# Output projection of two convolution layers: one fp32 product, or three fp32r products of split operands

## The reference

```python
p = silu(x @ p_w.T + p_b); q = silu(x @ q_w.T + q_b); v = silu(x @ v_w.T + v_b)
a1 = rpe_mlp(pos, t1) * decay        # taps of a Toeplitz product along w, one set per channel
a2 = rpe_mlp(pos, t2) * decay        # the same along h
qv = q * v
out = p * (toeplitz_w(qv, a1) + toeplitz_h(qv, a2))
x = x + (out @ o_w.T + o_b)          # o_w: (192, 576); this product is what the change touches
```

## Time and profile before

| | us |
|---|---|
| median of the runs | 19111.07 |
| profiled execution | 19115.89 |
| its span | 19114.2 |
| PE busy | 14621.5 (76%) |
| DVE busy | 13659.7 (71%) |
| ACT busy | 9805.9 (51%) |
| POOL busy | 7607.1 (40%) |

### The profile page before, as it was taken

How to read it: one execution, slowest core, us unless ns; L and a number is a source line. 1 busy time by engine, 2 the same in 40 slices (tenths; PEclk the granted TensorE clock), 3 DMA queues, 4 the chain that set the end, 5 groups by cost and what they waited for, 6 DMA issues and landing times. The chain is left out here.

```text
span 19114.2 us, 278580 instructions
## 1 busy us (share of the span) xinstructions
PE 14621.5 (76%) x79256; PEld 8486.3 (44%) x79256; DVE 13659.7 (71%) x13058; ACT 9805.9 (51%) x14679; POOL 7607.1 (40%) x4057
## 2 busy tenths in 40 slices
PE   7899898989997677767676776677777667767789
PEld 5666666666665333333233333333333333333367
DVE  5666666666665788778688778688787688787732
ACT  4444444444443566565366556266665356665400
POOL 1000000000000477666366666177666366666500
PEclk9999999999998899999899999899999889999999
DMA  5222222222222000000100000100000100000011
GB/s 122 59 59 59 63 51 62 58 64 56 56 59 67 14 4 1 3 4 13 42 2 3 3 4 1 54 1 3 4 1 3 48 7 4 3 1 3 28 47 40
DMA packets 127667, 562.53 MB, mean 29 GB/s; under 512 B 20988, under 2 KB 81788, under 8 KB 105468
## 3 DMA queue, kind: packets, MB, share of 16 engines
q1 hardware_dynamic: 114780, 470.00, 10.0%
q0 software_dynamic: 12288, 86.71, 2.1%
HBM read 440.00 MB, written 126.27 MB: 30 GB/s over the span
## 5 line engine op out<-in xcount | busy, mean ns | idle before, releaser
L1156 POOL TENSOR_TENSOR L2.u<-L2.u 128x784 f32<-128x784 f32 x3072 | 5656.9, 1849 | 1821.7 <-PE L2.ps L1261 1233.6
L1261 PE MATMUL L2.ps<-L2.u,L2.ident 128*128 128x392 f32 x12288 | 4595.7, 499 | 129.4 <-DVE L2.y L1618 129.4
L1630 DVE TENSOR_TENSOR_SCAN L2.u<-L2.u,L2.state,L2.ps 128x784 f32<-128x784 f32 x2304 | 4163.1, 1834 | 175.5 <-ACT L2.ps L1413 146.9
L1419 ACT COPY L2.u<-L2.ps 128x784 f32<-128x784 f32 x3840 | 3102.9, 808 | 902.7 <-PE L2.ps L1230 895.9
L1230 PE MATMUL L2.ps<-L2.bs,L2.sel 96*128 (+3 forms) x6144 | 1626.8, 352 | 2204.1 <-DVE L2.u L1630 925.5
L1413 ACT ACTIVATE L2.u<-L2.d,L2.nega 128x784 f32<-128x784 f32 x2304 | 2190.7, 951 | 2144.0 <-DVE L2.u L1630 1969.0
L1261 PEld LDWEIGHTS L2.ps<-L2.u,L2.ident 128*128 128x128 f32 x12288 | 2177.5, 192 | 1402.5 <-DVE L2.y L1618 186.1
L1605 DVE TENSOR_TENSOR L2.ps<-L2.ps,L2.du 128x784 f32<-128x784 f32 x2304 | 2215.1, 969 | 719.2 <-PE L2.ps L1230 701.0
L1230 PE MATMUL L2.ps<-L2.cs,L2.sel 96*128 96x392 bf16 (+1 forms) x6144 | 1628.8, 348 | 704.4 <-ACT L2.u L1419 672.3
L1230 PEld LDWEIGHTS L2.ps<-L2.bs,L2.sel 96*128 x6144 | 541.9, 101 | 3067.6 <-issue 2854.6
L1145 POOL TENSOR_TENSOR L2.u<-L2.u,L2.du 128x784 f32<-128x784 f32 x768 | 1410.9, 1837 | 1190.1 <-ACT L2.u L1419 1190.1
(11 more groups left out here) (231 smaller groups left out, 21259.3 us busy)
## 6 DMA issues: line engine op xcount, KB each, us to landing
L0.left<-table SPq DMA_DIRECT2D x48, 1176.0 KB
L0.right<-table SPq DMA_DIRECT2D x48, 1176.0 KB
L1.left<-table SPq DMA_DIRECT2D x48, 1176.0 KB
L1.right<-table SPq DMA_DIRECT2D x48, 1176.0 KB
table<-taps POOLq DMA_DIRECT2D x24, 1176.0 KB, 15.8
L0.wg<-L_w SPq DMA_DIRECT2D x49, 433.5 KB, 3.5
L1.wg<-L_w SPq DMA_DIRECT2D x49, 433.5 KB, 3.5
L0.x_res<-x POOLq DMA_DIRECT2D x8, 2352.0 KB, 13.4
```

Source lines behind the costliest of these rows:

```text
L1156: pool.tensor_tensor(hc[:, n % RING, :], hs[:, n % RING, :], cb[n % RING], ALU.mult)\
L1261: mm = pe.matmul(ps[:, 6 + h, 0:HSPAN], ident[:], hc[:, n % RING, h * HSPAN:(h + 1) * HSPAN], start=(n % STATES == 0), stop=(n % STATES == ...
L1419: act.copy(out.rearrange("p (a n) -> p a n", a=2), ps[:, 4:6, 0:HSPAN]).then_inc(c_out, 1)
L1630: dve.tensor_tensor_scan(hs[:, n % RING, :], a, b, state[:, n:n + 1], ALU.mult, ALU.add).then_inc(scanned, 1)
```

## The change

The product by `wo` is no longer one fp32 product. `wo` is split into `wo_hi` and `wo_lo` once per iteration, on POOL. Each chunk of `po` is split into `po_hi` (a copy to fp32r on ACT) and `po_lo` (a subtraction on POOL). PE then makes three fp32r products per half: hi by hi, low weight by high data, high weight by low data. `po` and its parts have three slots, and `turn_back` and `times_p` stand two chunks ahead.

```diff
@@ -183,7 +183,11 @@
         w_lo = m.sb("w_lo", [HALF, 2 * 3 * HALF], F32R)
         bias = m.sb("bias", [HALF, 3])
         wo = m.sb("wo", [HALF, CH])
-        po = m.sb("po", [HALF, 2, CHUNK])
+        wo_hi = m.sb("wo_hi", [HALF, CH], F32R)
+        wo_lo = m.sb("wo_lo", [HALF, CH], F32R)
+        po = m.sb("po", [HALF, 3, CHUNK])
+        po_hi = m.sb("po_hi", [HALF, 3, CHUNK], F32R)
+        po_lo = m.sb("po_lo", [HALF, 3, CHUNK], F32R)
         ident = m.sb("ident", [HALF, HALF])
         gmean = m.sb("gmean", [HALF, HALF])
         ob = m.sb("ob", [HALF, 2])
...
@@ -311,6 +318,20 @@
                         pool.wait_ge(skewed, 32 * (g + 1))
                     pool.sem_inc(tables_made, 1)
 
+            def split_shares(b):
+                with pool.Fori(0, GROUPS) as g:
+                    it = pool.snap(b * GROUPS + g)
+                    po0 = pool.snap(it * NCHUNK)
+                    pool.wait_ge(wo_in, it * 16 + 16)
+                    steady(pool)
+                    pool.tensor_copy(wo_hi[:], wo[:]).then_inc(wo_split, 1)
+                    pool.wait_ge(wo_split, it * 2 + 1)
+                    pool.tensor_tensor(wo_lo[:], wo[:], wo_hi[:].bitcast(F32), ALU.subtract).then_inc(wo_split, 1)
+                    for t in range(NCHUNK):
+                        pool.wait_ge(hi_done, po0 + (t + 1))
+                        pool.tensor_tensor(po_lo[:, t % 3, :], po[:, t % 3, :], po_hi[:, t % 3, :].bitcast(F32),
+                                           ALU.subtract).then_inc(lo_done, 1)
+
             load(0)
             make_tables(range(1))
             pool.wait_ge(const_in, 48)
@@ -320,11 +341,14 @@
             if later is not None:
                 for g in range(GROUPS):
                     skew(pool, g, *later, skewed)
+            split_shares(0)
             with pool.Fori(1, BATCH - 1) as b:
                 add_bias(b)
                 pool.wait_ge(x_stored, b * 16 + 16)
                 load(b + 1)
+                split_shares(b)
             add_bias(BATCH - 1)
+            split_shares(BATCH - 1)
             if later is not None:
                 pool.wait_ge(skewed, 2 * 32 * GROUPS)
 
@@ -406,7 +430,8 @@
 
                     for s in range(2):
                         pe.wait_ge(toe_done[s], toe0 + HTOES)
-                    pe.wait_ge(wo_in, it * 16 + 16)
+                    pe.wait_ge(wo_split, it * 2 + 2)
+                    lo0 = pe.snap(it * NCHUNK)
 
                     def turn_back(t):
                         if t >= 2:
@@ -418,17 +443,20 @@
                         mm.then_inc(turn_ready, 1)
 
                     def share(t):
-                        pe.wait_ge(po_done, po0 + (t + 1))
+                        pe.wait_ge(lo_done, lo0 + (t + 1))
                         for j in range(2):
 
                             pe.wait_ge(added, added0 + (2 * t + j - 1 if t else 0))
-                            pe.matmul(p_out[0:HALF, j, 0:CHUNK], wo[:, j * HALF:(j + 1) * HALF], po[:, t % 2, :],
-                                      start=True, stop=True).then_inc(out_ready, 1)
+                            for q, (w, p) in enumerate(((wo_hi, po_hi), (wo_lo, po_hi), (wo_hi, po_lo))):
+                                mm = pe.matmul(p_out[0:HALF, j, 0:CHUNK], w[:, j * HALF:(j + 1) * HALF], p[:, t % 3, :],
+                                               start=(q == 0), stop=(q == 2))
+                            mm.then_inc(out_ready, 1)
 
                     turn_back(0)
+                    turn_back(1)
                     for t in range(NCHUNK):
-                        if t + 1 < NCHUNK:
-                            turn_back(t + 1)
+                        if t + 2 < NCHUNK:
+                            turn_back(t + 2)
                         share(t)
 
         @block.scalar
@@ -479,6 +507,13 @@
                         copy_toeplitz(act.copy, n).then_inc(toe_done[0], 1)
                     for t in P_SUMMED:
                         silu_p(t)
+                    po0 = act.snap(it * NCHUNK + 1)
+                    out0 = act.snap(it * SHARES + 1)
+                    for t in range(NCHUNK):
+                        act.wait_ge(po_done, po0 + (t + 1))
+                        if t >= 3:
+                            act.wait_ge(out_ready, out0 + (2 * t - 4))
+                        act.copy(po_hi[:, t % 3, :], po[:, t % 3, :]).then_inc(hi_done, 1)
 
         @block.vector
         def _(dve):
@@ -573,8 +608,8 @@
                         dve.wait_ge(silu_done, silu0 + (2 * NCHUNK + t + 1))
                         dve.wait_ge(turn_ready, turn0 + (TURNS + t + 1))
 
-                        dve.wait_ge(out_ready, out0 + max(2 * t - 2, 0))
-                        dve.tensor_tensor(po[:, t % 2, :], p_back[0:HALF, t % 2, 0:CHUNK],
+                        dve.wait_ge(out_ready, out0 + max(2 * t - 4, 0))
+                        dve.tensor_tensor(po[:, t % 3, :], p_back[0:HALF, t % 2, 0:CHUNK],
                                           p_all[:, t * CHUNK:(t + 1) * CHUNK], ALU.mult).then_inc(po_done, 1)
 
                     def add_share(t):
@@ -584,10 +619,11 @@
                             dve.tensor_tensor(place, place, p_out[0:HALF, j, 0:CHUNK], ALU.add).then_inc(added, 1)
 
                     times_p(0)
+                    times_p(1)
                     dve.wait_ge(biased, b * 2 + 2)
                     for t in range(NCHUNK):
-                        if t + 1 < NCHUNK:
-                            times_p(t + 1)
+                        if t + 2 < NCHUNK:
+                            times_p(t + 2)
                         if t == 1:
                             take_weights(it + 1)
                         add_share(t)
```

More of the change, by code:

```diff
@@ L227, in tno_layer @@
         po_done = m.sem("po_done")
+        hi_done = m.sem("hi_done")
+        lo_done = m.sem("lo_done")
+        wo_split = m.sem("wo_split")
         out_ready = m.sem("out_ready")
```

## The result

| | before | after |
|---|---|---|
| median of the runs, us | 19110.43 | 19758.86 |
| lowest and highest | 19107.91, 19123.44 | 19753.68, 19766.29 |
| ratio, 95% interval | | 1.0338, 1.032 to 1.0356 |

The account below looks back on a forecast made before the run. PE was taken to bound the kernel, in the tail too. From 19115.9 us profiled, -5 for the tails and +132 for the first image gave 19243, or 19238 for the median (0.66% slower), with a range of 19170 to 19355.

Parts of the forecast that it names:

- the tail's term: Tail of each iteration in layers 0 and 1: 17.56 us against 17.61, -0.05 us, times 96 about -5 us.
- Its upper bound, 17.77 plus 0.3 us: Tail with POOL's subtraction at 1.31 us, 0.3 us to start, another 0.3 of unknown latencies: +0.45 us, +43 us.
- the first-image term: First image, layer 0: PE waits once for POOL's splits behind the table DMAs; +132 us, 2 for PE's clock included.
- the prediction's own signs of being wrong: No gap in the first image, or a tail under 16.5 or over 18.5 us; layer 1 iterations expected unchanged.
- DVE held by POOL: Tail: POOL delays `take_weights` on DVE by up to 1.25 us; +115 us, total 19353; chance 0.14.
- The rival of a cheap first image: First image: POOL through its table DMAs 70 us sooner, near 250 us; total 19202; chance 0.10.
- The faster rival: Tail: PE's own work alone decides, 15.0 us, 2.5 less, -240 us; total 19003; chance 0.02.

Follow-up runs that it names:

- x2: The changed kernel with five discarded fp32r matmuls on PE ahead of `share(0)`; 19591.36 us, 72 of 96 tails fall.
- x1: The changed kernel with POOL's first-image program reordered, so that each group's splits stand between the table DMAs; 19625.84 us, all 96 tails fall.
- x4: The changed kernel without copies and splits, three fp32r matmuls per half taken from `xt`, true output projection left out; 19258.09 us, 58 of 96 tails fall.
- x9: x7 with five discarded matmuls per tail: three ahead of `share(2)`, one each ahead of `share(5)` and `share(6)`; 18978.4 us, no tail falls.
- x8: The kernel before with only `turn_back` and `times_p` two chunks ahead and `po` in three slots, old fp32 product; 19569.28 us, 55 of 96 tails fall.
- x5: x4 with `turn_back` and `times_p` one chunk ahead, as in the kernel before; 19308.71 us, 70 of 96 tails fall.
- x3: The changed kernel with both splits and their waits kept, but the product again one fp32 product; 20119.62 us, all 96 tails fall.
- x10: x9 with one more discarded matmul each ahead of `share(1)`, `share(3)` and `share(4)`; 19046.33 us, no tail falls.
- x11: x8 with `turn_back(0)` and `turn_back(1)` between the p projections as in x7; 19116.9 us, no tail falls.
- x12: The changed kernel in its own order with 15 discarded matmuls per tail, five ahead of `share(0)`, none between `turn_back`s; 19644.18 us, 55 of 96 tails fall.
- x13: The changed kernel in its own order with 13 discarded matmuls per tail, five of them behind the first two `turn_back`s; 19627.27 us, 41 of 96 tails fall.
- x7: x1 with the first two `turn_back`s between the p projections and ACT's first two copies between its silus; 19166.57 us, 48 of 96 tails fall.

## Why the prediction was wrong

**The step that failed** is the tail's term, -0.05 us a tail. Its working took every matmul at the pace of the full clock. Its upper bound, 17.77 plus 0.3 us, was made of latencies and left the clock out, though the first-image term allowed 2 us for it. The tail measured 22.4 to 23.6 us, +5.4 us a tail in place of -0.05. The missed mechanism is PE's granted clock: 0.99 for the first 5.57 us of the tail shown, 0.50 for the other 17.05. It falls in all 96 tails of after. The projections behind the tail shown run at full speed. Two of the prediction's own signs of being wrong are there: a tail over 18.5 us, and iterations of layer 1 that are longer than before (61.1 us in the median, against 56.0).

**At full clock the working held.** A tail of x2 that stays, with the chain and the product of after, takes 17.46 us where 17.56 were forecast. Its fillers put `share(0)` 0.15 us later than in after, so the tail of after at full clock could be a little shorter. The saving against before is 0.07 us, about 7 us in all, where 5 was forecast. The parts, with the forecast in brackets: the copy on ACT 0.565 us (0.57), the subtraction on POOL 1.14 (1.25), `share(0)` at 3.49 (3.66), a chunk at 2.2 (2.2).

**The first image** held: 133.16 us of wait against 132 in all, and x1 gives 133 back. POOL was through its table DMAs at 286.6 us, where 284 was forecast. The place was wrong: the wait stands in front of `turn_back(0)`, which needs the split of `wo`, and not in front of `share(0)`, which comes only at 291.33, where 287 was forecast. The sum comes out within 2 us in part by luck, since the 2 us allowed for the clock help to cover that. No run shows those 2 us as a cost of the wait: the clock is down in that first tail as in all 96.

**The rivals.** DVE held by POOL did not happen. `take_weights` kept its cast of 0.60 and its subtraction of 0.76 us; DVE went first, and POOL was the one held, 1.63 instead of 1.14 us. The rival of a cheap first image had POOL through near 250 us; it was 286.6. The faster rival named 2.5 us a tail. x4, with no chain at all, saves 1.1 and keeps 1.1 us of waits for DVE; x9 saves 1.35 an iteration. So the rival failed on the chain, on DVE's adds and on the clock. Neither a rival nor the range, which ended at 19355, held a slow clock. It was priced nowhere, though the prediction's own figures allow it: 42 matmuls at twice 0.204 us are 8.6 us more a tail at most.

**What brings the clock down, as far as shown.** The new order (x8), the new product without its chain (x4, x5), and the chain with the old product (x3) each bring it down, the last in every tail, the others in 55 to 70 of 96. Filling the wait ahead of `share(0)` (x2) frees 24 tails; turning back between projections and filling the waits of `share(2)`, `share(5)` and `share(6)` (x9) frees all. So what stands in a tail, and its waits, set how many moments are bad ones: every one that was reached in after, x1 and x3, none that was reached in x9, x10 and x11, and in before one tail in 96, behind a longer wait. Among tails of one kernel, the moment at which a tail arrives sets whether it falls. That is why only some fall, and by patterns that repeat with the images. It would also explain x5's spread from run to run, which is argued: three of its four runs have no trace.

The Trainium skill bears on this in "TensorE: Matmul & The Clock Gate". By Part 4, transposes don't count as PE being busy in the way matmuls do. The clock of the tail shown above falls 5.7 us after its start, and four `turn_back`s of 0.8 us, which the code writes as transposes, fill 3.2 of these; the rule fits. But x9 has the same number of `turn_back`s and never falls, and no run shows how they are counted. By Part 1, the number of slow matmuls at the start of one kernel varies from run to run, with where the activity monitor stands when the kernel starts. x5's 173 us between lowest and highest would fit this, deep inside a kernel.

**What stays open** is why the changed order with its waits filled (x12 but for 0.23 us, x13 wholly) still has bad moments where x10, in x9's order, has none. x9 has one long projection ahead of its first `turn_back`s and two behind, the others three ahead and only fillers behind. That this is the reason was not tried.

## What to carry to other kernels

Before costing a PE stretch at full speed, ask whether the change gives it short waits, or puts rows of small transposes where long matmuls stood, and price the stretch at half clock as a rival. Afterwards read the granted clock by stretch before looking for a wait: here PE was busy 17.05 of 17.05 us, and the time was in the pace. Moving useful work into a wait gained most (x7, 459 us less than x1), and a few discarded matmuls can pay on top (x9: five a tail, 188 us less than x7). Runs of one program that spread like x5's are a sign that some of its stretches fall and others don't. An order that shows no fall in one trace may not have met every moment; x10's margin costs 68 us over x9.

## What the runs showed of the hardware

- Once down, the clock stayed at 1.2 GHz though PE was busy without a gap: 17.05 us in after, and in x13 from the middle of the fillers almost to the tail's end.
- Of the same instructions with PE always busy, some tails ran at 2.4 GHz and some fell to 1.2 (x13: 55 and 41 of 96), separated by the moment at which they start, with two misplaced.
- A 448-column fp32r copy from SBUF to SBUF on ACT took 565 ns, where one out of PSUM took 526. POOL's two-input operation took 1.14 us for 448 columns, where the line through the earlier trace rows gives 1.31.
- Where `take_weights` and POOL's subtraction met, DVE's 0.76 us subtraction was not slowed and POOL's was (1.63 us instead of 1.14).
- Beside POOL's DMA issues, from 213.43 us of before on, DVE's bias copy and its cast of 864 columns took 0.94 and 1.32 us, where they take 0.15 and 0.60.
